# Two-layer language tower: in the first layer all scores ahead in TensorE's step, maximum and subtraction ahead of DVE's embedding work, values projected once

## The reference, cut to what matters

```python
h = _L0_tok_ref(...)                       # tok_w[ids] + pos_w + type_w, LayerNorm, gamma, beta
x = _layernorm(h)
q = (x @ Wq.T + bq) * SCALING; k = x @ Wk.T + bk; v = x @ Wv.T + bv
# per batch column and head, over the 64 positions of the first axis:
scores = einsum('bqd,bkd->bqk', q, k)
attn = einsum('bqk,bkd->bqd', softmax(scores), v)
h = h + attn @ Wout.T + bout
h = h + moe_ffn(_layernorm(h))             # 8 experts, 2 per token
h = h + L1_attn(_layernorm(h)); h = h + L1_ffn(h)
```

## Time and profile before

| | us |
|---|---|
| median of 3 runs | 2254.14 |
| lowest, highest | 2242.58, 2262.70 |
| the profiled execution, device time | 2241.71 |
| its span, first to last instruction | 2239.7 |
| layer 0's steady stretch, looked at below | 120 to 560 us of the span |

### The profile page before, as it was taken

One profiled execution on the slowest core, in us unless ns is written; L12 is line 12 of the kernel. 1 busy time (PEld: TensorE's weight loads), 2 busy tenths in 40 slices (PEclk: granted clock), 3 DMA queues, 4 the chain that ended last, 5 costly groups with the idle time before them and its releaser, 6 DMA issues. The chain is left out here.

```text
span 2239.7 us, 55751 instructions
## 1 busy us (share of the span) xinstructions
PE 1826.0 (82%) x17448; PEld 1643.8 (73%) x17448; DVE 1393.2 (62%) x3156; ACT 1198.7 (54%) x3343; POOL 579.3 (26%) x1168
## 2 busy tenths in 40 slices
PE   4989888989500047999999999689999999999985
PEld 4777777777400047999999999678888888888872
DVE  6777777777432233455455554377888888788735
ACT  3777777777300012333333333378878787887821
POOL 4433333342047710000000000223333333333100
PEclk9999999999655578999999999889999999999957
DMA  4221212121012259788888888465655565566513
GB/s 134 60 63 57 63 56 59 60 58 41 12 53 78 77 162 277 225 234 238 234 232 239 236 235 232 123 193 170 175 171 170 171 174 172 167 174 173 157 31 112
DMA packets 377513, 321.95 MB, mean 144 GB/s; under 512 B 55450, under 2 KB 338542, under 8 KB 377454
## 3 DMA queue, kind: packets, MB, share of 16 engines
q1 hardware_dynamic: 357790, 287.49, 44.7%
q0 software_dynamic: 15360, 31.48, 4.8%
q10 hardware_dynamic: 4304, 2.23, 0.4%
HBM read 209.51 MB, written 111.60 MB: 143 GB/s over the span
## 5 line engine op out<-in xcount | busy, mean ns | idle before, releaser
L1138 ACT ACTIVATE prob<-ps_s,b1s 128x256 f32<-128x256 f32 x432 | 181.3, 471 | 369.0 <-PE ps_s L1122 369.0
L1122 PE MATMUL ps_s<-xhi,w1hi_c 128*128 128x256 f32 x864 | 239.3, 295 | 2.6 <-DVE xhi L1160 2.6
L1122 PE MATMUL ps_s<-xhi,w1lo_c 128*128 128x256 f32 x864 | 229.5, 283 | 0.0
L1152 DVE CAST w1hi_c<-score 128x768 fp32r<-128x768 f32 x144 | 74.1, 557 | 229.0 <-DMA score<-w1h 229.0
L1097 PE MATMUL ps_v<-probT,prob 128*128 128x192 f32 x864 | 213.4, 329 | 0.0
L1097 PE MATMUL ps_k<-probT,prob 128*128 128x192 f32 x864 | 213.0, 329 | 0.0
L378 PE MATMUL ps_q<-xT,wqk_c 128*128 128x128 f32 x1536 | 211.7, 290 | 1.4 <-ACT xT L609 1.4
L1085 PE MATMUL ps_t<-ident,xs 128*128 128x128 f32 x144 | 38.5, 293 | 207.7 <-DMA score<-w1h 206.8
L378 PEld LDWEIGHTS ps_q<-xT,wqk_c 128*128 128x128 f32 x1536 | 191.1, 199 | 4.1 <-ACT xT L609 2.3
L431 PEld LDWEIGHTS ps_v<-vv,probT 128*128 128x128 f32 x1536 | 189.0, 198 | 1.1 <-issue 1.0
L431 PE MATMUL ps_v<-vv,probT 128*128 128x17 f32 x1536 | 187.6, 261 | 0.5 <-DVE hres L677 0.5
(11 more groups left out here) (209 smaller groups left out, 4761.6 us busy)
## 6 DMA issues: line engine op xcount, KB each, us to landing
rel_d<-rpad SPq DMA_DIRECT2D x64, 864.0 KB, 4.4
relb<-rel_d SPq DMA_DIRECT2D x64, 768.0 KB, 4.6
probT<-w2h SPq DMA_DIRECT2D x72, 576.0 KB, 4.2
score<-w1h SPq DMA_DIRECT2D x72, 384.0 KB, 3.3
score<-w1h SPq DMA_DIRECT2D x144, 192.0 KB, 3.9
xs_d<-zrow SPq DMA_DIRECT2D x64, 216.0 KB, 2.9
xs<-xs_d SPq DMA_DIRECT2D x72, 192.0 KB, 2.5
ys_d<-ys SPq DMA_DIRECT2D x72, 192.0 KB, 5.0
```

The costliest lines, as they stand in the source:

```text
L1122: last = pe.matmul(dst, w, x, start=(k == 0), stop=(k == len(terms) - 1))
L1138: last = act.activation(hT[b][:, c, :], ps_s[:, j, (c % 2) * BLK:(c % 2) * BLK + BLK], ACT.Gelu, bias=b1s[b][:, c:c + 1])
L1152: ch.step(dve.tensor_copy(w1hi[b][c][:], w1[b][c]))
```

## The change

Four edits, all in layer 0:

1. PE: all 12 heads' scores (48 records of L363 and as many weight loads) stand at the start of the step; the second half behind `out_project` is gone.
2. DVE: the maximum of the scores stands first in the step, then `xn`, then the subtraction, then `embed_and_normalise` and `outputs`. Behind `outputs` now comes `zn` with its two copies, and then the reciprocal. In layer 1 the order is what it was; the code is only moved into two functions.
3. PE: one value projection in place of two; ACT's four value copies read `ps_v` of the partitions 64c and write the partitions 64s, so two of the four cross partitions.
4. ACT: `xT0` and `xT1` are 128 wide and the two copies L606 and L607 are gone.

```diff
-        xT0 = two("xT0", [128, 192])
-        xT1 = two("xT1", [128, 192])
+        xT0 = two("xT0", [128, 128])
+        xT1 = two("xT1", [128, 128])
...
-                    last = pe_project(pe, ps_v[:, 0:D], xT0[b][:, 0:128], xT1[b][:, 0:128], v_w[l])
-                    if l == 0:
-
-                        last = pe_project(pe, ps_v[:, D:2 * D], xT0[b][:, 64:192], xT1[b][:, 64:192], v_w[l])
-                    last.then_inc(S["v_ps"], 1)
+                    pe_project(pe, ps_v[:, 0:D], xT0[b][:], xT1[b][:], v_w[l]).then_inc(S["v_ps"], 1)
...
-                    for j in range(H // 2):
+                    for j in range(H if l == 0 else H // 2):
                         scores(j)
...
-                if st.has("s"):
+                if l == 1 and st.has("s"):
                     for j in range(H // 2, H):
                         scores(j)
...
-                        pv = ps_v[:, 0:2 * D].rearrange("p (w r s e) -> p w r s e", w=2, r=H // 2, s=2)
+                        pv = ps_v[:, 0:D].rearrange("p (r s e) -> p r s e", r=H // 2, s=2)
                         for c in range(2):
                             for s in range(2):
 
                                 ins = act.activation(vb[64 * s:64 * s + 64, c, :, s, 0:DH],
-                                                     pv[64 * s:64 * s + 64, 0 if s == c else 1, :, s, :], ACT.Copy)
+                                                     pv[64 * c:64 * c + 64, :, s, :], ACT.Copy)
...
-                    if l == 0:
-                        act.activation(xT0[b][:, 128:192], ps_t[:, 0:64], ACT.Copy)
-                        act.activation(xT1[b][0:D1, 128:192], ps_t[0:D1, 128:192], ACT.Copy)
...
+                if l == 0:
+                    found = maxima()
                 if st.has("xn"):
...
                 if l == 0:
+                    subtract_maxima(found)
                     if st.has("emb") or st.has("ln"):
                         embed_and_normalise()
...
                 outputs()
...
+                if l == 1:
+                    found = maxima()
                 if st.has("z"):
...
+                if l == 1:
+                    subtract_maxima(found)
                 if st.has("o"):
```

More of the change, by code:

```diff
@@ L378, in queries_keys @@
                     last = pe.matmul(ps_q[:, o:o + 128], qk_w[l][chunk][:, o:o + 128],
-                                     (xT0, xT1)[chunk][b][:, 0:128], start=(chunk == 0), stop=(chunk == 1))
+                                     (xT0, xT1)[chunk][b][:], start=(chunk == 0), stop=(chunk == 1))
                     if j == 2 * SLOTS - 1:
@@ L604, in body @@
                     after(act, S["zT_ps"], done("z"))
-                    if l == 0:
-                        act.activation(xT0[b][:, 128:192], ps_t[:, 0:64], ACT.Copy)
-                        act.activation(xT1[b][0:D1, 128:192], ps_t[0:D1, 128:192], ACT.Copy)
-                    act.activation(xT0[b][:, 0:128], ps_t[:, 0:128], ACT.Copy)
-                    act.activation(xT1[b][0:D1, 0:128], ps_t[0:D1, 128:256], ACT.Copy).then_inc(S["xT_sb"], 1)
+                    act.activation(xT0[b][:], ps_t[:, 0:128], ACT.Copy)
+                    act.activation(xT1[b][0:D1, :], ps_t[0:D1, 128:256], ACT.Copy).then_inc(S["xT_sb"], 1)
                 if st.has("z"):
@@ L677, in outputs, with maxima, subtract_maxima @@
                     dve.tensor_tensor(h, ps_v[:, 0:D], h, ALU.add).then_inc(S["y_ok"], 1)
+                def maxima():
+                    if not st.has("s"):
+                        return None
+                    b = st.two("s")
+                    sc = score[b][:, :, :, 0:keys]
+                    psv = ps_s[:, :, 0:A * keys].rearrange("p g (a k) -> p g a k", a=A)
+                    dve.wait_ge(S["s_ps"], done("s"))
+                    if l == 0:
+                        src = psv
+                    else:
+                        dve.wait_ge(M_["rld"][b], 16 * (st.pair("s") + 1))
+                        dve.tensor_tensor(sc, psv, relb[b][:].rearrange("p (g a) k -> p g a k", g=G),
+                                          ALU.add).then_inc(S["s_rd"], 1)
+                        dve.wait_ge(S["s_rd"], done("s"))
+                        src = sc
+                    ch.link(dve.tensor_reduce(mx[b][:].rearrange("p (g a) -> p g a", g=G), src, AX.X, ALU.max))
+                    return sc, src
+                def subtract_maxima(found):
+                    if found is None:
+                        return
+                    sc, src = found
+                    b = st.two("s")
+                    m4 = mx[b][:].rearrange("p (g a o) -> p g a o", g=G, o=1).to_broadcast([128, G, A, keys])
+                    dve.tensor_tensor(sc, src, m4, ALU.subtract).then_inc(S["s_sub"], 1)
+                if l == 0:
+                    found = maxima()
                 if st.has("xn"):
```

## The result

| | us |
|---|---|
| median after (4 runs) | 2329.2 (2322.2 to 2333.0) |
| median before, runs of the same comparison (4) | 2254.2 |
| ratio, 95% interval | 1.0344 (1.0314 to 1.0375) |
| span of the profiled execution | 2320.5, before 2239.7 |

The account below looks back on a forecast made before the run. DVE and POOL waiting for each other in each step of layer 0 bound the kernel, PE following; 56 steps at 1.00 + 0 + 0.20 + 0.33 = 1.53 us, less 4, gave +82 us: 2334 us, range 2300 to 2374.

Parts of the forecast that it names:

- What bounds the kernel: Layer 0 step: DVE and POOL wait for each other, 8.41 us in the timeline, 8.63 mean; PE follows.
- The maximum, +1.00 us a step: DVE, layer 0: moved from POOL's shadow to the stretch from `zn` to `mvb`, it costs +1.00 us a step.
- The subtraction, 0: DVE, layer 0: its 0.87 us moves from before `xn` to after it, both in the loop, so 0.
- DVE's wait for the scores, +0.2: DVE, step start: maximum can start 1.80 us after `zn`, DVE free at 1.56; +0.2 us a step, ends 0 and 0.6.
- the 0.6 that would have shown the forecast wrong: Sign in the new profile: the maximum's wait for the scores above 0.6 us would make the forecast wrong.
- The gap and the clock, +0.33: PE ahead of the sums: 2.4 us idle each step lowers the clock; +0.33 us a step, ends 0 and 1.3.
- One value projection, 0 in the steady part and -4 in the drain: PE, layer 0: 0.63 us less a step, worth 0 in steady steps, -4 us in all from drain and start.
- ACT, 0: ACT, layer 0: two copies fewer, two crossing partitions at 0.01 us a copy; nothing in the loop waits, so 0.
- The sum: Layer 0: 56 steps at 1.53 us more, 86, less 4, is +82 us; step from 8.63 to about 10.2.
- Rival A: PE is the bound and the change is faster: 1.07 us a step gained, median 2190 us; chance 0.04.
- Rival B: Clock low for most of PE's critical section: 2.2 to 2.5 us a step, +128, median 2382 us; chance 0.15.
- Rival C: The maximum alone costs, no wait for scores and no clock loss: +52, median 2306 us; chance 0.13.

Follow-up runs that it names:

- the filled run: Changed kernel plus eight unread matmuls on PE in the gap ahead of the sums: 2315.4 us, ratio 1.0298 to the kernel before.
- the first experiment: Changed kernel with DVE's maximum and subtraction moved back to their old places: 2260.8 us, ratio 1.0060 to the kernel before.
- the run with two projections: Changed kernel with DVE's old order and a second, unread value projection on PE: 2255.1 us, ratio 1.0020 to the kernel before.

## Why the prediction was right, point by point

- *What bounds the kernel.* Right, and shown: moving a square root on POOL gains 2.0% in the kernel before, an instruction in front of `xn` costs 0.83 us a step, and the same instruction behind `outputs` 0.1 us in three steps of four (45 against 18 us over the whole kernel).
- *The maximum, +1.00 us a step.* Right: 1.00 us from its start to `xn`. The added maximum, whose result nobody waits for, takes 0.83; it reads another tile, but the subtraction, which reads the same one and is not waited for either, takes 0.87. So of the 1.00 the wait on its own result is some 0.13 to 0.17 us. The part that it left stayed at 2.69 us, 0.07 below the old 2.76, which I had not counted.
- *The subtraction, 0.* Right: 0.87 us at either place.
- *DVE's wait for the scores, +0.2.* Too small. With the clock full the maximum starts 2.06 us after `zn` in the step shown, not 1.80. The last score starts a little earlier than in my sum (1.51 us after `zn`, forecast 1.63), but from there to the maximum it is 0.55 us, and my sum had 0.17, what is left of 0.46 behind 0.39, and a tenth for the signal. In the four steps at full clock the maximum starts 0.14 to 0.60 us after the 1.56 at which DVE would be free, about 0.4 a step. In the changed kernel's own trace, low clock included, the wait is 22.2/43 = 0.52 us, near the 0.6 that would have shown the forecast wrong.
- *The gap and the clock, +0.33.* A long gap does come, the clock falls behind it, and its mean fell from 0.98 to 0.83. But the gap is not 2.4 us in every step, as forecast, and the wait is not above 2 us a step: it is 2.2 to 2.8 us in 19 of 43 steps and 1.50 on the mean, because after a fall PE comes late and has hardly a gap. The size is about right by difference: 10.20 us is the mean step, and the filled run has 9.91 at full clock; that leaves 0.29. That it lies so near 0.33 is luck in part, since the forecast took a quarter of a full price of 1.3 us and no row gave the quarter. The runs that change the clock alone agree in direction (10 us in the changed kernel, 56 with POOL reordered).
- *One value projection, 0 in the steady part and -4 in the drain.* Right: the drain is 4.5 us shorter, and 5.4 longer again with the second projection back. That the missing work could cost something by way of the clock was argued for PE's gap as a whole; the pair of runs in DVE's old order points to it for the projection alone.
- *ACT, 0.* The waits name ACT ahead of PE's transposes of the probabilities 16 times for 6.2 us in all, before 39 times for 11.7, and ahead of none of DVE's instructions; its two copies that cross partitions were not measured by themselves.
- *The sum.* 56 steps by 1.57 us measured (10.20 - 8.63) are 88 us, forecast 86; less the drain. The wait for the scores came out 0.2 above its term, the clock 0.04 below and the stretch from `mvb` to `zn` 0.07 below, so part of the close total is errors that offset each other; the mean step before holds a few steps at low clock of its own, so the terms don't add up more closely than that.

Rival A is refuted by four runs (DVE's order undone, the second projection, the maximum in front, POOL's order in the kernel before). Rival B had its mechanism right and its size wrong: the clock falls in about every second step and not in each one, since in the time at the low clock PE's next gap all but closes. The prediction's range also went only to 2374 us, below the 2382 that it had worked out for B. Rival C is out by the wait for the scores.

What stays open: the 13 us of the first experiment in full, as 4 to 6 of them are left in the run with two projections, inside its interval, and how much of the changed kernel's 75 us the clock has in it exactly, since the filling that would show it also delays the sums where the clock is low.

## What to carry to other kernels

Add up the loop in which two engines wait for each other before believing shares of busy time: here POOL, busy 37% of layer 0's steady stretch, and DVE, busy 75%, set the step, and PE at 90% followed. One and the same maximum cost 0.1 us where its engine waits for the other one, and 0.83 us elsewhere on the loop; so before an instruction is moved to remove a wait, see what it covers where it stands. And look at the order on the idle engine first: to serve the value that is ready before those that are still being made was worth 2.0% alone and 3.0% together with the lighter PE, but nothing that can be told in the changed kernel, until the clock was held up there.

## What the runs showed of the hardware that I had not expected

- Work taken off an engine with slack can lower its clock and seems to cost time. With one projection less on PE the granted clock of layer 0's steady stretch went from 0.97 to 0.88 and the kernel was 0.4% slower by the ratios, with intervals that just touch, in the same order of all else.
- The low clock need not come in the gap itself. In the step shown it came about a microsecond after the end of 2.70 us of idle time, stayed for 6.9 us in which PE was busy throughout, and so took away the next gap (0.36 us).
- The filling of PE's gap with eight unread matmuls raised the clock from 0.79 to 1.00 and gained 56 us of 2318, about as much as the reordering of POOL at full clock (54). Where the loop over POOL was closed it gained 10 us.
- A DVE maximum of 128x768 lasts 0.92 to 0.96 us, but moves its successor by 0.83 when nothing waits for its result (it reads a constant tile there), and by 1.00 when something does (it reads the scores).
